# A coupled feed-forward stage: its signed feature exchange by DMA instead of by matrix products

## The reference, cut to what matters

```python
def _coupling_net(h, w1, b1, w2, b2, w3, b3, w4, b4):     # 128 -> 128 -> 64 -> 32 -> 1
    h = _gelu(h @ w1 + b1); h = _gelu(h @ w2 + b2); h = _gelu(h @ w3 + b3)
    return jax.nn.sigmoid(h @ w4 + b4)

def _twist(x):
    o_r, o_i, p_r, p_i = jnp.split(x, 4, axis=-1)
    return jnp.concatenate([p_r, -p_i, -o_r, o_i], axis=-1)

out = x                                                   # x: 8192 rows of 128 features
for _ in range(3):
    tf = _coupling_net(out, ...)
    combined = 0.7 * gf + 0.3 * tf                        # gf: one value for each sequence
    coupling = 0.1 + adaptive_range * (combined - 0.5) * 2.0
    out = out + coupling * _twist(out)
```

## Time and profile before

| | |
|---|---|
| median of 3 runs | 7063.54 us (7063.35 to 7069.24) |
| the profiled execution's own time | 7066.77 us |
| its span, first to last instruction | 7065.0 us |
| mean granted TensorE clock | 0.972 of 2.4 GHz |
| slots 0 to 46 of this stage | 1860 to 2068 us |

### The profile page before, as it was taken

The page is one execution under the profiler, slowest core; times in us unless marked ns, Lnnn a source line. Parts: engine busy times, 40 slices in busy tenths (PEclk is TensorE's granted clock), DMA queues, the critical chain, the costliest instruction groups (busy, mean ns, idle before and its releaser), DMA issues. The chain is left out here.

```text
span 7065.0 us, 179781 instructions
## 1 busy us (share of the span) xinstructions
PE 6395.6 (91%) x70180; PEld 3908.0 (55%) x70180; DVE 5368.1 (76%) x9382; ACT 4036.3 (57%) x6084; POOL 2793.1 (40%) x1672
## 2 busy tenths in 40 slices
PE   7989988988778999899999789898999999989999
PEld 5767675444423333333333356576577777766677
DVE  7868577777459999999999966587677777768544
ACT  4556344776347777777777555464344444456433
POOL 3312175434118888888888401264022222222000
PEclk9999999999789999999999999899999999999999
DMA  1000000000002222222222100100000000000000
GB/s 30 0 21 13 3 12 8 3 3 2 14 13 75 78 75 77 80 75 72 75 75 75 45 8 12 38 0 3 13 2 2 2 2 2 2 16 14 8 9 9
DMA packets 115298, 188.37 MB, mean 27 GB/s; under 512 B 38421, under 2 KB 74458, under 8 KB 114394
## 3 DMA queue, kind: packets, MB, share of 16 engines
q1 hardware_dynamic: 112666, 182.23, 8.1%
q10 hardware_dynamic: 2240, 0.53, 0.1%
HBM read 172.74 MB, written 7.86 MB: 26 GB/s over the span
## 5 line engine op out<-in xcount | busy, mean ns | idle before, releaser
L2640 POOL TENSOR_TENSOR m_dBx<-m_dtx,m_Bs 128x1024 f32<-128x1024 f32 x512 | 1159.6, 2284 | 244.1 <-DVE m_hs L3018 197.2
L3018 DVE TENSOR_TENSOR_SCAN m_hs<-m_ps_dA,m_dBx 128x512 f32<-128x512 f32 x1024 | 1193.3, 1207 | 67.0 <-POOL m_dBx L2640 55.2
L2765 PE MATMUL m_ps_y<-m_yc,ident 128*128 128x512 f32 x2048 | 1021.9, 622 | 0.0
L2875 ACT ACTIVATE m_ps_dA<-m_dt,m_A 128x504 f32<-128x504 f32 x1024 | 679.7, 678 | 453.2 <-DVE m_hs L3018 450.2
L2138 POOL TENSOR_TENSOR a_s<-a_s,a_den 128x1024 f32<-128x1024 f32 x128 | 243.7, 1904 | 1110.7 <-DVE a_den L2184 1110.7
L3029 DVE TENSOR_TENSOR m_yc<-m_hs,m_ps_C 128x1024 f32<-128x1024 f32 x512 | 612.6, 1196 | 2.6 <-PE m_ps_C L2746 2.3
L2765 PEld LDWEIGHTS m_ps_y<-m_yc,ident 128*128 128x128 f32 x2048 | 349.6, 190 | 357.8 <-issue 357.5
L2746 PE MATMUL m_ps_C<-m_parts,m_sel 48*128 48x512 bf16 x512 | 199.1, 389 | 189.0 <-DVE m_yc L3029 189.0
L2746 PEld LDWEIGHTS m_ps_C<-m_parts,m_sel 48*128 48x128 bf16 x512 | 47.4, 92 | 581.0 <-DVE m_yc L3029 439.4
L643 POOL TENSOR_TENSOR c_kbd<-c_kf,c_hmask 128x1024 f32<-128x1024 f32 x66 | 125.1, 1895 | 503.4 <-ACT c_kf L552 485.3
L2182 DVE TENSOR_REDUCE a_den<-a_s 128x16 f32<-128x1024 f32 x128 | 156.1, 1219 | 204.0 <-ACT a_s L2089 204.0
(11 more groups left out here) (752 smaller groups left out, 15771.2 us busy)
## 6 DMA issues: line engine op xcount, KB each, us to landing
m_Bs<-BC_rows SPq DMA_DIRECT2D x256, 512.0 KB, 3.6
c_kvb<-in_ctxT SPq DMA_DIRECT2D x68, 128.0 KB, 2.1
c_kvb<-in_ctxT SPq DMA_DIRECT2D x17, 256.0 KB, 2.6
out_dram<-X SPq DMA_DIRECT2D x16, 256.0 KB, 2.3
BC_rows<-m_low SPq DMA_DIRECT2D x32, 64.0 KB, 2.8
part_rows<-m_split SPq DMA_DIRECT2D x32, 48.0 KB, 1.7
m_parts<-part_rows SPq DMA_DIRECT2D x32, 48.0 KB, 1.7
c_table<-in_table SPq DMA_DIRECT2D x2, 512.0 KB, 3.3
```

Of the source, the lines that this page charges most:

```text
L2640: return nc.gpsimd.tensor_tensor(to, one, other, ALU.mult)
L2765: last = nc.tensor.matmul(ps_y[:, m, :], C.ident[:], of[:, m, :], start=s == 0, stop=s == NS - 1)
L2875: nc.scalar.activation(seqs(ps_dA[:, h % 3, :]), seqs(dt[:, par, m, :]), ACT.Exp, scale=A[:, second, m, s:s + 1]).then_inc(decay, 1)
L3018: nc.vector.tensor_tensor_scan(hs[:, s % HS, m, :], ps_dA[:, (2 * s + m) % 3, :], dBx[:, s % BX, m, :], 0.0, ALU.mult, ALU.add).then_inc(s ...
```

## The change

The products with `perm` go. In their place SP copies the two halves of `cur[:, q]` crosswise into a new SBUF tile `partner[:, q]`, by two DMAs of 64 partitions x 1024 fp32 (256 KB) for each update. They are issued at `l` = 0, as soon as `cur` is final for the cycle, and are needed at `l` = 4. The sign of each feature is a column `sign`, multiplied once into the scaling columns `reach3`, `reach7` and a new `tenth`, so that `tt` after `blend` already has the sign of the term. `update` multiplies by `partner` (SBUF) where it read `bank` (PSUM).

```diff
+            def partners(q, r, c):
+                if c == 0:
+                    sp.wait_ge(cur_ready[q], r + 1)
+                if r + c:
+                    sp.wait_ge(updated[q], r * CYCLES + c)
+                for half in range(2):
+                    to, of = slice(S * half, S * half + S), slice(S - S * half, 2 * S - S * half)
+                    sp.dma_start(partner[to, q, :], cur[of, q, :]).then_inc(partnered[q], 16)
+            for t in slots:
+                for j, n in steps(t):
+                    q, r, c, l = counts(j, n)
+                    if 0 < n < STEPS - 1 and l == 0:
+                        partners(q, r, c)
...
-            def twist(q, done):
-                pe.wait_ge(l_act[q], done)
-                for e in range(2):
-                    last = nc.tensor.matmul(bank[:, q, e, :], perm[:], cur[:, q, e * GT:(e + 1) * GT], start=True, stop=True)
-                last.then_inc(perm_done[q], 1)
...
-            ts(reach3[:], reach[:], 0.3, None, ALU.mult)
-            ts(reach7[:], reach[:], 0.7, None, ALU.mult)
+            ts(reach3[:], reach[:], 0.3, sign[:, 0:1], ALU.mult, ALU.mult)
+            ts(reach7[:], reach[:], 0.7, sign[:, 0:1], ALU.mult, ALU.mult)
+            ts(tenth[:], sign[:], 0.1, None, ALU.mult)
...
-                dve.wait_ge(perm_done[q], r * CYCLES + c + 1)
-                tensor(tt[:, q, :], tt[:, q, :], bank[:, q, :, :].rearrange("p e n -> p (e n)"), ALU.mult)
+                dve.wait_ge(partnered[q], 32 * (r * CYCLES + c + 1))
+                tensor(tt[:, q, :], tt[:, q, :], partner[:, q, :], ALU.mult)
...
-                    ts(gain[:], gain[:], reach7[:, 0:1], 0.1, ALU.mult, ALU.add)
+                    ts(gain[:], gain[:], reach7[:, 0:1], tenth[:, 0:1], ALU.mult, ALU.add)
```

More of the change, by code:

```diff
@@ L2225, in coupled_shapes @@
     return dict(w0=[P, P], w1=[P, S], w2=[P, 32], w3=[S, P], b0=[P, 1], b1=[P, 1], b2=[S, 1], b3=[P, 1], gw0=[P, S], gw1=[S, 32],
-                gw2=[32, P], gb0=[S, 1], gb1=[32, 1], gb2=[P, 1], perm=[P, P], reach=[P, 1], pick=[P, 2])
+                gw2=[32, P], gb0=[S, 1], gb1=[32, 1], gb2=[P, 1], sign=[P, 1], reach=[P, 1], pick=[P, 2])
 def coupled_loads(t, W):
-    plain = [(t[k][:], W[k]) for k in ("pick", "gw0", "gw1", "gw2", "gb0", "gb1", "gb2", "w0", "w1", "b0", "b3", "perm", "reach")]
+    plain = [(t[k][:], W[k]) for k in ("pick", "gw0", "gw1", "gw2", "gb0", "gb1", "gb2", "w0", "w1", "b0", "b3", "sign", "reach")]
     return plain + [(t["w2"][0:S, :], W["w2"]), (t["w2"][S:P, :], W["w2"]), (t["w3"][0:32, :], W["w3"]), (t["w3"][32:S, :], W["w3"]),
@@ L2251, in coupled_ffn @@
         gb0, gb1, gb2 = sb("gb0", [S, 1]), sb("gb1", [32, 1]), sb("gb2", [P, 1])
-        perm, reach, pick = sb("perm", [P, P]), sb("reach", [P, 1]), sb("pick", [P, 2])
-        reach3, reach7 = sb("reach3", [P, 1]), sb("reach7", [P, 1])
+        sign, reach, pick = sb("sign", [P, 1]), sb("reach", [P, 1]), sb("pick", [P, 2])
+        reach3, reach7, tenth = sb("reach3", [P, 1]), sb("reach7", [P, 1]), sb("tenth", [P, 1])
         rs_pick, nm_pick = sb("rs_pick", [P, C.NT, 2]), sb("nm_pick", [P, C.NT, 2])
@@ L2257, in coupled_ffn @@
         cur, h0, h1, h2 = sb("cur", [P, NSET, PC]), sb("h0", [P, NSET, PC]), sb("h1", [P, NSET, GT]), sb("h2", [S, NSET, GT])
-        tt = sb("tt", [P, NSET, PC])
+        tt, partner = sb("tt", [P, NSET, PC]), sb("partner", [P, NSET, PC])
         st = sb("st", [P, PT, 6])
@@ L2264, in coupled_ffn @@
         xn_ready = sem("xn_ready")
-        xT_done, cur_ready, back_done, back_read, l_done, l_act, blended, perm_done, updated = (
+        xT_done, cur_ready, back_done, back_read, l_done, l_act, blended, partnered, updated = (
             [sem(f"{n}{q}") for q in range(NSET)] for n in
-            ("xT_done", "cur_ready", "back_done", "back_read", "l_done", "l_act", "blended", "perm_done", "updated"))
+            ("xT_done", "cur_ready", "back_done", "back_read", "l_done", "l_act", "blended", "partnered", "updated"))
         scales = NormScales(C, sc, 1e-5)
@@ L2367, in _ @@
                         layer3(q, done)
-                    else:
-                        twist(q, done)
                 if t == 0:
@@ L4217, in constants @@
     c["table_a3"] = twice(bias).reshape(P, 4, UH, S)
[L4218 to L4222, removed]
+    c["partner_sign"] = np.repeat(np.array([1, -1, -1, 1], np.float32), D // 4)[:, None]
     c["pick_mean"] = (row[:, None] // S == np.arange(2)[None, :]).astype(np.float32) / S
@@ L4383, in focus_and_coupled @@
     names = [f"{k}{n}" for k, m in (("w", 4), ("b", 4), ("gw", 3), ("gb", 3)) for n in range(m)]
-    f1 = pick(A, "f1_", perm="perm", reach="reach", pick="pick_mean", **{n: n for n in names})
+    f1 = pick(A, "f1_", sign="partner_sign", reach="reach", pick="pick_mean", **{n: n for n in names})
     return x1, f1
```

## The result

In 20 runs each, the change takes 7078.8 us in the median and the kernel before 7067.7; the ratio is 1.0017, 95% interval [1.0011, 1.0023], so 8 to 16 us slower, against +6.0 forecast. The profiled execution has a span of 7079.5 us. I measure the changed stage by itself, from the first product of slot 0 to the end of the last statistics of slot 46: 207.9 us before, 215.15 after, +7.25. After the stage both kernels take the same (4996.8 and 4996.5 us). Slot 0 itself begins 7.6 us later (1867.81 against 1860.24). All that the change touches ahead of it is one load and a few instructions on single columns, and the kernel before, profiled once more, began slot 0 at 1869.35, so this start scatters.

A forecast was written before the change was run, and what follows sets the result against it. The prediction took DVE's chain, not PE, to bound the stage. Its terms -7.2 + 2.0 + 8.5 + 2.7 summed to +6.0 us, giving 7069.5 us, own range 7060 to 7077, whole range 7056 to 7087.

The forecast's parts named there:

- slots 5 to 8, DVE no longer waits for the twist: Slot 5: DVE's 1.8 us wait for PE's `perm` product (the twist) goes, of which 1.0 us was taken as gain.
- port +2.0: Slots 9 and 10: DVE instructions with two SBUF inputs slow down beside POOL, +2.0 us, bounds 0 and 2.96.
- clock +1.7: Slots 10, 15, 19, 36, 41: after each long PE rest, half-rate work costs 2.7 us, 1.0 hidden, so +1.7 each.
- slots 22 to 34, -4.0 and clock +2.7: Staggered part: earlier updates and `leave` win 4.0 us by slot 34's `layer3`; one or two slow-clock rests cost 2.7.
- last cycle: Pair 7's blend is done 2.26 us before the `perm` product lets DVE's product start; 2.2 us taken as gain.
- The rival in which PE was the bound: Whole stage: all or at least half of PE's 43 us comes back, 7020 to 7042 us; chance 0.08.
- The gain, -7.2: Whole stage: without the `perm` products on PE, DVE no longer waits for them in four places, -7.2 us together.
- The product reads SBUF, +2.0: `update`'s product: free at rest with SBUF input, but slower beside POOL in slots 9 and 10, +2.0 us.
- The clock, +8.5 + 2.7 = 11.2: PE's longer rests lower its clock: +8.5 us in five places, +2.7 in the staggered part; bounds 0 and 28.
- The copies, 0: SP's copies for each update take 3.6 to 7.6 us, covered by some 11 us before the product needs them: 0.
- The first rival, the clock paid in full: Each of eight rests costs 3.5 us, or `layer1` to `layer3` also fall to 1.2 GHz: +23, 7086 us; chance 0.28.

The follow-up runs named there:

- product_from_psum: The changed kernel without the copies, its product reading `bank` (PSUM), so the exchange of halves is left out: stage 209.5 us, 182.3 from slot 8.
- filler_in_place: The changed kernel plus a product nobody reads on PE where the removed `perm` product was: stage 208.9 us, ratio 1.0004 to the kernel before.
- no_copies: The changed kernel without the 48 copies, its product reading `cur` in SBUF, so the exchange of halves is left out: stage 215.0 us.
- all_three: The changed kernel with POOL later, update directly behind its blend, and unread products in PE's rests: stage 192.0 us, ratio 0.9977 to the kernel before.
- pool_later_after: The changed kernel with POOL making `xn` of pairs 3 to 7 only after bursts of DVE work: stage 197.3 us, ratio 0.9997 to the kernel before.

## Why the prediction was right

The time, +6.0 us forecast, was +11 by the runs and +7.25 in the stage. 7078.8 us lies in the whole range (7056 to 7087), but over the 7060 to 7077 that I gave the forecast itself. What bounds the stage was read rightly, while two of the terms were far off, and it is luck that they offset. Place by place, as the walk had it, and by how much later each `layer3` came:

| place | forecast | measured |
|---|---|---|
| slots 5 to 8, DVE no longer waits for the twist | -1.0 | +0.8 |
| slots 9 to 13, port +2.0 and clock +1.7 | +3.7 | +5.0 |
| slot 15, clock | +1.7 | +1.25 |
| slot 19, clock | +1.7 | +0.9 |
| slots 22 to 34, -4.0 and clock +2.7 | -1.3 | -0.9 |
| slot 36, clock | +1.7 | 0.0 |
| slot 41, clock | +1.7 | +2.0 |
| last cycle | -2.2 | -1.85 |
| sum | +6.0 | +7.25 |

- **DVE's chain, not PE, is the bound.** Shown: 43 us of PE work went and the stage grew longer all the same. PE's idle time in it rose from 22.7 to 57.2 us, and its `layer0`s took 15.7 us more. The rival in which PE was the bound is out. One reading behind it was wrong: the 26.4 us of waits added the wait of the weight loads to that of the products, but both are the same time, and 26.4 is more than all of PE's idle time in the stage. Against DVE's 7.3 us stood 9.6 of the products, or 16.8 of the weight loads, so the evidence was thinner than it looked.
- **The gain, -7.2.** Of it 6.2 were for places from slot 8 on. With POOL out of the way and the rests filled, 174.9 us from there on became 166.5, -8.4: some 4.7 ahead of the last cycle (4.0 forecast) and 3.8 in it (2.2 forecast). In that last cycle a part is the clock once more, since without fillers `layer3` took 1.55 us there for 1.13 and the twist 3.78 for 1.98. So the mechanism was right and the size close. Slot 5's part (-1.0) was lost to POOL: the place came out at +0.8.
- **The product reads SBUF, +2.0.** This is the term that was most off. Beside POOL a product took 2.76 us with two SBUF inputs and 1.22 with one. The Trainium skill states this as a rule (SBUF — State Buffer, Who interferes with whom): a DVE instruction with two SBUF inputs contends with a GpSimd instruction that reads SBUF, and the trace agrees in kind. But I priced only what was newly slow, and put slot 5 at nothing. The change costs 6.4 us from slot 8 on with POOL in its place and gains 1.6 with POOL out of the way (174.9 to 173.3), so POOL's part is 8.0 us. Of these 3.0 come from the product's input (product_from_psum). The other 5.0 I read as blends and additions that were slow before too, but under PE's work, and now are on the chain. This is worked out from differences, not measured by itself, and a part of it is clock: with POOL later the `layer0`s have 3.9 us less of slow time.
- **The clock, +8.5 + 2.7 = 11.2.** Shown by itself at 6.8 us with POOL out of the way, and at 6.3 with POOL in its place, where slot 10 stayed slow (filler_in_place). The `layer0` behind the rest of slot 36 was slow as forecast, 3.75 us, but it was hidden entirely: behind the first `layer0` came `leave` and another wait for DVE.
- **The copies, 0.** They landed in 3.7 us in the median (3.1 to 5.3), well under the 7.6 taken as the most; no_copies shows 0.1 us.
- The two errors, port too small by 6 and clock too large by 4, offset each other, which nothing in the prediction foresaw. The sum was nearer than its terms. And the terms are not quite separate: -8.4, 8.0 and 6.8 add up to the measured 6.4 because each was taken as a step between two kernels, and in another order the steps would differ.

The first rival, the clock paid in full, did not come, since half of the slow work is hidden.

## What to carry to other kernels

Where PE is full and yet waits briefly for another engine at each turn, work taken from PE turns into rests; price them at the clock that they cost, and see first which queue sets the turn. When a filler engine goes, recount every instruction that it had covered, not only the edited ones: the blends had been slow all along. By the whole kernel's time the change paid only when what it made possible was used (the update directly behind its blend), with POOL moved off DVE's bursts and PE's rests filled. And compare it then with a kernel before that has the same help: POOL's later start, for one, helps there too.

## What the runs showed of the hardware

- Rests of 2 to 3 us cost the granted clock in some places and not in others. In the change it stayed at 1.00 through 3.05 us without work before 2000.92 and in the `layer0`s behind it (first row below; the 5.78 us have 0.1 us of waiting in them), while `layer0` took 3.78 us after 3.54 us of rest in slot 23 and 3.23 after 2.96 in slot 32. In slot 10 of filler_in_place the clock fell behind a rest of 2.24 us.

```profile
2000.92 5.78 PE L2332 MATMUL f_bank<-f_cur,f_w 128*128 128x512 f32 x12 [3.05 <-DVE f_cur L2469]
...
1980.26 3.78 PE L2332 MATMUL f_bank<-f_cur,f_w 128*128 128x512 f32 x4 [3.54 <-DVE f_cur L2469]
```

- Both sides slow down where DVE and POOL meet in SBUF: DVE's product and addition took 2.76 us for 1.22, POOL's two passes 2.25 to 2.27 and 2.69 for 1.90 (slots 5 and 9 of the change).
- The moment at which the clock rises after the slow start of the stage differs between kernels whose code is the same up to there: the `layer3` of slot 4 came at 1.2 GHz (2.08 us) in all_three and at 2.4 (1.13) in pool_later_after, both on one chip. It moved the rest of the stage by 2 to 4 us, as much as the things under study. The two profiles of the same kernel agreed in it, for the kernel before and for the change; what decides it is not shown.
- Fp32 products that nobody reads, 1.8 us each step, made a stage shorter by 6.3 us, against the same kernel without them.
